# State-space heads: chunks along the free axis, two heads on the partition halves, two pairs multiplied in turn

## The reference

```python
proj = hidden @ W_in * mup_vector                  # 256 -> 1344
z, xBC, dt = split(proj, [512, 512 + 768])
xBC = silu(conv_b + causal 4-tap convolution of xBC along time)
x, Bm, Cm = xBC[:512] as 64 heads x 8, xBC[512:640], xBC[640:]
dt = softplus(dt + dt_bias)                        # one per head and step
dA = exp(dt * -exp(A_log))
state = state * dA_t + (dt_t * x_t) (outer) B_t    # per head: 8 x 128
y_t = state . C_t                                  # 512 steps, 64 heads
y = (y + D * x) * silu(z); y *= rsqrt(mean(y^2) + eps) * norm_w
out = y @ W_out
```

## Time and profile before

| | us |
|---|---|
| median of 3 runs | 1537.1 |
| the profiled execution, its own time | 1533.86 |
| its span, first to last instruction | 1532.1 |
| layer norm 2, 750 to 770 | 20 |
| projection stage, 770 to 884 | 114 |
| heads stage, 884 to 1229 | 345 |
| mean granted TensorE clock | 0.91 |

### The profile page before, as it was taken

How to read it: one execution, slowest core, us unless ns; L and a number is a source line. 1 busy time by engine, 2 the same in 40 slices (tenths; PEclk the granted TensorE clock), 3 DMA queues, 4 the chain that set the end, 5 groups by cost and what they waited for, 6 DMA issues and landing times. The chain is left out here.

```text
span 1532.1 us, 35054 instructions
## 1 busy us (share of the span) xinstructions
PE 1224.8 (80%) x13688; PEld 930.2 (61%) x13688; DVE 991.7 (65%) x2104; ACT 613.6 (40%) x1380; POOL 618.5 (40%) x540
## 2 busy tenths in 40 slices
PE   2789898988854999997168778989888846999992
PEld 1356665656542889886134336666666635989882
...
GB/s 149 148 133 155 186 163 168 169 181 151 122 67 139 420 341 235 248 220 43 154 1 3 12 15 2 2 3 2 2 2 2 2 84 324 415 233 251 234 123 175
DMA packets 93702, 209.91 MB, mean 137 GB/s; under 512 B 33057, under 2 KB 64546, under 8 KB 87394
## 3 DMA queue, kind: packets, MB, share of 16 engines
...
## 5 line engine op out<-in xcount | busy, mean ns | idle before, releaser
L1222 ACT ACTIVATE ffn_h<-ffn_bank,ffn_b 128x256 f32<-128x256 f32 (+1 forms) x384 | 144.2, 430 | 274.5 <-PE ffn_bank L118 267.5
L2208 POOL TENSOR_TENSOR ssm_GL<-ssm_L,ssml_G 128x512 f32<-128x512 f32 x128 | 164.7, 1295 | 109.7 <-DVE ssm_L L2117 109.7
L1399 DVE CAST ffn_hh<-ffn_h 128x512 f16<-128x512 f32 (+1 forms) x192 | 73.6, 383 | 179.0 <-ACT ffn_h L1222 169.8
L1034 POOL DMA_INDIRECT ffn_xs<-xn_rows,ffn_from_rows x78 | 78.2, 1003 | 266.3 <-PE ffn_bank L1117 180.8
L116 PE MATMUL ffn_bank<-ffn_hh,ffn_W 128*128 128x256 f16 (+1 forms) x768 | 180.2, 253 | 4.9 <-DVE ffn_hl L1401 4.9
L117 PE MATMUL ffn_bank<-ffn_hl,ffn_W 128*128 128x256 f16 (+1 forms) x768 | 180.0, 252 | 0.0
L118 PE MATMUL ffn_bank<-ffn_hh,ffn_W 128*128 128x256 f16 (+1 forms) x768 | 180.0, 252 | 0.0
L1973 PE MATMUL ssm_Y<-ssm_GL,ssmh_windows 64*32 64x64 f32 x4096 | 145.5, 223 | 9.4 <-POOL ssm_GL L2208 9.0
L2117 DVE TENSOR_TENSOR_SCAN ssm_L<-ssm_bank,ssmh_ident 128x512 f32<-128x512 f32 x128 | 151.1, 1210 | 0.8 <-PE ssm_bank L1956 0.8
L1973 PEld LDWEIGHTS ssm_Y<-ssm_GL,ssmh_windows 64*32 64x32 f32 x4096 | 124.6, 111 | 38.1 <-issue 24.7
L642 ACT ACTIVATE att_prob<-att_bank,att_nmax 128x512 f32<-128x512 f32 (+3 forms) x256 | 127.2, 525 | 29.4 <-DVE att_nmax L724 28.1
...
...
## 6 DMA issues: line engine op xcount, KB each, us to landing
...
att_piece<-in_ffn_w SPq DMA_DIRECT2D x32, 512.0 KB, 5.0
split_w<-att_halves SPq DMA_DIRECT2D x32, 512.0 KB, 4.3
...
ffn_back<-y_rows SPq DMA_DIRECT2D x16, 512.0 KB, 7.3
att_KB<-att_krl SPq DMA_DIRECT2D x8, 512.0 KB, 5.5
...
xn_rows<-ffn_XN SPq DMA_DIRECT2D x8, 512.0 KB, 2.6
```

What stands on the lines that cost most here:

```text
L1222: ins_ = act.activation(h[layer][:, m, 0:n], bank[1 + 2 * layer + u][:, (m % 2) * n:(m % 2 + 1) * n], ACT.Gelu, bias=bias[:, ds(e + m, 1)])
L2208: pool.tensor_tensor(GL[:, p % RING, :, :, :].rearrange("p x i n -> p x (i n)"), L[:, p % RING, :, :, :].rearrange("p x i n -> p x (i n)") ...
```

## The change

Heads stage. The eight chunks of time now lie along the free axis, and the two halves of the partitions hold the two heads of a pair. So a product in `multiply` runs over all 128 rows. `multiply` is called for every second p and takes two pairs at once, with products of 128 rows x 32 columns that alternate between two column groups. `scan` writes into one ring of 6 slots (4 new, 2 in the no longer needed `FT`), and `mult` works in place there. `windows` has 3 slots and is filled by two ACT instructions for each pair. `update` becomes two products of half the width on the two halves of the partitions, in two banks. The tables `finishes` and `outputs` have other numbers.

Projection stage. x, dt and the suffix decays now have to come out with head halves on the partitions. The transposes become ordinary float32 products with picked columns of the identity, 64 x 64 each, and `multiply_g` is cut into 64 x 64 pieces too. B is stored to DRAM by SP and loaded again in the heads stage, in the new layout. The weights are permuted on the host to match. The decays go to `piece` by 8 DMAs instead of 32.

Elsewhere. In `layer_norm_stage` DVE normalises group g + 1 before the low parts of group g - 1. In `ffn_stage` SP waits for the gathered rows of tile 0 before it loads the second part of the first expert, and for those of tile 1 before it goes on to the other experts.

```diff
             statistics(1)
+            normalise(0)
             for g in range(G):
-                normalise(g)
                 if g + 2 < G:
                     statistics(g + 2)
+                if g + 1 < G:
+                    normalise(g + 1)
...
                     sp.dma_start(to[:, :, 0:W2_AT], src[:, :, 0:W2_AT]).then_inc(first_in, 16)
+                    sp.wait_ge(xs_loaded[0], 32)
                     sp.dma_start(to[:, :, W2_AT:], src[:, :, W2_AT:]).then_inc(weights[0], 16)
+                    sp.wait_ge(xs_loaded[1], 32)
...
                 for i in range(TB):
-                    one = slice(i * P, (i + 1) * P)
-                    ins = pe.matmul(bank[7][:, one], bc[:, one], CT[:, b * TB + i, :], start=True, stop=True)
+                    for par in range(2):
+                        at = slice((2 * i + par) * CH, (2 * i + par + 1) * CH)
+                        for x in range(2):
+                            ins = pe.matmul(bank[7][half(x), at], bc[:, at], CT[:, b * TB + i, par * CH:(par + 1) * CH], start=True, stop=True)
                 ins.then_inc(s["g_psum"], 1)
...
-                    for c in range(XB):
-                        ins = pe.transpose(bank[5 + i % 2][:, c * P:(c + 1) * P], xc[:, c, i * P:(i + 1) * P], identf[:, :])
+                    for par in range(2):
+                        for c in range(XB):
+                            at = (par * XB + c) * CH
+                            for x in range(2):
+                                ins = pe.matmul(bank[5 + i % 2][half(x), at:at + CH], xc[:, c, i * P + par * CH:i * P + (par + 1) * CH],
+                                                channels[:, x, :, :], start=True, stop=True)
                     ins.then_inc(s["xt_psum"], 1)
...
+            def turn_by_heads(rows, before, chunks_read):
 
                 pe.wait_ge(s["xt_done"], 2 + chunks_read)
                 pe.wait_ge(s["turned"], before)
                 for r in range(PAIRS):
+                    for c in range(2 * TB):
+                        for x in range(2):
+                            ins = pe.matmul(bank[5 + r][half(x), c * CH:(c + 1) * CH], rows[:, r * S + c * CH:r * S + (c + 1) * CH],
+                                            heads[:, x, :, :], start=True, stop=True)
+                    ins.then_inc(s["turn_psum"], 1)
+
...
+            def store_b(b):
+                sp.wait_ge(s["b_done"], b + 1)
+                sp.dma_start(b_rows[b].rearrange("(i p) n -> p i n", p=P), Bt[:, :, :]).then_inc(s["b_stored"], 16)
+
+            def spread_halves(part, src):
+                for r in range(PAIRS):
+                    for bb in range(2):
+                        sp.dma_start(piece[part * SH:(part + 1) * SH, 2 * r + bb, :], src[bb * SH:(bb + 1) * SH, r, :]).then_inc(s["pieces"], 16)
+
+            for b in range(B - 1):
+                store_b(b)
+            sp.wait_ge(s["hi_done"], 1)
+            spread_halves(0, hi16)
+            sp.wait_ge(s["lo_done"], 1)
+            spread_halves(1, lo16)
+            store_b(B - 1)
+            sp.wait_ge(s["pieces"], 4 * PAIRS * 16)
+            sp.wait_ge(s["b_stored"], 16 * B)
+
...
-    RING, WINDOWS = 3, windows.shape[1]
+    RING, WINDOWS, YB = 6, windows.shape[1], 3
...
-        L, GL = sb("L", [P, RING, 2, TB, CH]), sb("GL", [P, RING, 2, TB, CH])
-        edtx, states = sb("edtx", [P, 2, SD]), sb("states", [P, NC - 1, SD])
+        L = sb("L", [P, RING - B // 2, S])
+        slots = [L[:, n, :] for n in range(RING - B // 2)] + [FT[:, r, :] for r in range(B // 2)]
+        Bt = sb("Bt", [P, 2, NC, P])
+        edtx, states = sb("edtx", [P, 2, 2, SD // 2]), sb("states", [P, NC - 1, SD])
         carried = sb("carried", [P, S - CH])
...
-        Y = ctx.enter_context(nc.psum_tensor("ssm_Y", [P, 4, 2, TB, CH], F32))
-        bank = t.banks(4)
+        Y = ctx.enter_context(nc.psum_tensor("ssm_Y", [P, YB, NC, CH], F32))
+        U = ctx.enter_context(nc.psum_tensor("ssm_U", [P, 2, S], F32))
+        bank = t.banks(3)
...
-        finishes = {PAIRS_B * b + at: (b, q) for b in range(B) for q, at in enumerate((19, 23, 40, 44) if b + 1 < B else (19, 23, 33, 34))}
-        outputs = {PAIRS_B * b + (49 if b + 1 < B else 39): b for b in range(B)}
+        finishes = {PAIRS_B * b + at: (b, q) for b in range(B) for q, at in enumerate((11, 19, 27, 35) if b + 1 < B else (11, 19, 27, 34))}
+        outputs = {PAIRS_B * b + (41 if b + 1 < B else 39): b for b in range(B)}
...
+            def load_b(b):
+                if b >= 2:
+                    sp.wait_ge(upd_psum, (b - 1) * (NC - 1))
+                for x in range(2):
+                    sp.dma_start(Bt[half(x), b % 2, :, :], b_rows[b].rearrange("(c t) n -> t c n", t=CH)).then_inc(bt_loaded[b % 2], 16)
...
-                for x in range(2):
-                    group, h = divmod(2 * m + x, SH // 2)
-                    ins = pe.matmul(bank[p % 2][:, x * TB * CH:(x + 1) * TB * CH], picks[:, h, :], piece[:, b, group, :], start=True, stop=True)
-                ins.then_inc(bc_ready, 1)
+                q, group, h = place(m)
+                pe.matmul(bank[p % 2][:, :], picks[:, q * PAIRS_Q + group * 2 + h, :], piece[:, b, :], start=True, stop=True).then_inc(bc_ready, 1)
...
-                if jj == 0 and q % 2 == 0 and b:
-
-                    pe.wait_ge(y_read, (b - 1) * XB + q + 2)
-                pe.wait_ge(window_done, p + 1)
-                pe.wait_ge(mult_done, p + 1)
-                for x in range(2):
-                    j = 2 * jj + x
-                    at, out_rows = AT - j % 4 * SP_, slice(j // 4 * GROUP, (j // 4 + 1) * GROUP)
-                    for i in range(TB):
-                        for par in range(2):
-                            rows = rows_of(par)
-                            ins = pe.matmul(Y[out_rows, q // 2 * 2 + par, q % 2, i, :], windows[rows, p % WINDOWS, x, i, at:at + GROUP],
-                                            GL[rows, p % RING, x, i, :], start=j % 4 == 0 and i == 0, stop=j % 4 == 3 and i == TB - 1)
+                q, _, h = place(m)
+                at = b * XB + q
+                if m % PAIRS_Q == 0 and at >= YB:
+
+                    pe.wait_ge(y_read, at - YB + 1)
+                pe.wait_ge(window_done, p + 2)
+                pe.wait_ge(mult_done, p + 2)
+                for c in range(NC):
+                    for n in range(2):
+                        group = place(m + n)[1]
+                        ins = pe.matmul(Y[group * GROUP:(group + 1) * GROUP, at % YB, c, :],
+                                        windows[:, (p + n) % WINDOWS, c, (1 - h) * SP_:(1 - h) * SP_ + GROUP],
+                                        slots[(p + n) % RING][:, c * CH:(c + 1) * CH], start=h == 0 and c == 0, stop=h == 1 and c == NC - 1)
                 ins.then_inc(y_done, 1)
 
             def update(b, c):
                 i, par = divmod(c, 2)
+                if c == 0:
+                    pe.wait_ge(bt_loaded[b % 2], (b // 2 + 1) * 32)
                 pe.wait_ge(edtx_done, b * TB + i + 1)
                 fourth_free()
-                pe.matmul(bank[3][:, :], Bt[rows_of(par), b * TB + i, :], edtx[rows_of(par), (b * TB + i) % 2, :], start=True,
-                          stop=True).then_inc(upd_psum, 1)
+                for x in range(2):
+                    ins = pe.matmul(U[:, x, 0:SD // 2], Bt[half(x), b % 2, c, :], edtx[half(x), (b * TB + i) % 2, par, :], start=True, stop=True)
+                ins.then_inc(upd_psum, 1)
                 used["update"] += 1
...
-                if 1 <= p <= NP:
-                    multiply(p - 1)
+                if 2 <= p <= NP and p % 2 == 0:
+                    multiply(p - 2)
...
-                    act.wait_ge(y_done, p - WINDOWS + 1)
-                act.activation(windows[:, p % WINDOWS, :, :, AT:AT + SP_].rearrange("p x i d -> p i x d"),
-                               dtx[:, b * TB:(b + 1) * TB, m * 2 * SP_:(m + 1) * 2 * SP_].rearrange("p i (x d) -> p i x d", x=2),
-                               ACT.Copy).then_inc(window_done, 1)
+                    act.wait_ge(y_done, (p - WINDOWS) // 2 + 1)
+                q, group, h = place(m)
+                at = (q * PAIRS_Q + group * 2 + h) * SP_
+                chunks = dtx[:, b * TB:(b + 1) * TB, :].rearrange("p i (a d) -> p (i a) d", a=2)
+                for x in range(2):
+                    ins = act.activation(windows[half(x), p % WINDOWS, :, (2 * x + 1) * SP_:(2 * x + 2) * SP_],
+                                         chunks[half(x), :, at:at + SP_], ACT.Copy)
+                ins.then_inc(window_done, 1)
...
-                    dve.wait_ge(mult_done, p - RING + 1)
-                dve.tensor_tensor_scan(flat(L[:, p % RING, :, :, :]), bank[p % 2][:, :], ident8[:, :], 0.0, ALU.mult,
+                    dve.wait_ge(y_done, (p - RING) // 2 + 1)
+                dve.tensor_tensor_scan(slots[p % RING], bank[p % 2][:, :], ident8[:, :], 0.0, ALU.mult,
```

(13 more changed lines are left out.)

171 lines of the change are left out of this document (92 added, 79 removed).

## The result

The changed kernel is slower: 1618.5 us (median of 4 runs, 1615.81 to 1620.21) against 1536.3, a ratio of 1.053 with a 95% interval of 1.050 to 1.056. The forecast was 1498. The profiled execution of the changed kernel has a span of 1616.0 us, 83.9 more than before.

What follows compares the result with a forecast made beforehand. In the heads, the loop through PE, DVE and POOL was taken to set the pace, not PE alone. Heads -41, projection +16, layer norms -6, FFN -6 gave -37 from the profiled 1533.9; forecast 1498 us, range 1462 to 1532.

Steps and rivals of the forecast that it cites:

- Layer norm: Layer norms 0 and 2: ACT's waits for DVE's shift go with DVE's order turned, -4.5 and -1.5, together -6 us.
- Mixtures of experts: FFN: weight loads put behind the gathers shorten PE's waits for gathered rows, -2.5 and -3.5, together -6 us.
- Projection: Projection stage: 33 us more PE work at 55 to 66 ns a turn_x record, partly covered, +16 us.
- Heads: Heads stage: two full batches -18, start -10, rest of batch 0 -5, last batch -8, together -41 us.
- the carry: Heads, carry period of two pairs: one round takes 5.5 us instead of 5.3; four in a full batch are 22.
- the update: Heads, update period of two pairs: falls from 4.37 to 3.5 us, what DVE needs; seven are 24.5, with squares 25.
- rival D: Heads: PE's clock stays at 0.50 through the stage, as PE is busy less; 1575 us, 6% chance.
- B: Heads: column groups do not run side by side, multiply takes 1.7 to 2.05 for two pairs; 1525 us, 15% chance.
- C: turn_x and multiply: load and product of a full-row record come one after the other; 1577 us, 6% chance.
- Rival E: Heads: deeper ring removes handovers, DVE and POOL set the pace, 60 us a batch; 1461 us, 15% chance.
- the eight pairs behind them: Heads, full batch: eight pairs after the four carry periods, with both halves of project, take 17.5 us.
- the rest: Heads, end of a full batch after the updates: 6.5 us, 6.1 before, by the later window.

Runs made afterwards that it cites:

- e_ln_ffn: Kernel before, with only DVE's new order in the layer norms and SP's two waits in the mixtures of experts: 1525.6 us against 1532.4.
- e_keep: Changed kernel with keep_decay ahead of window(p + 2) in ACT's order, nothing else changed: 1567.7 us.
- e_late_only: Changed kernel with spread(p + 2) behind multiply and update on PE in the even passes, nothing else changed: 1575.8 us.
- e_before_half: Kernel before with half of multiply's products left out, those of the second head of each pair: 1556.0 us against 1536.8.
- e_order: Changed kernel with keep_decay ahead of window and the even spread behind multiply and update, no idle products: 1519.4 us.
- e_same_group: Changed kernel with keep_decay ahead of window, three idle products a pass, and multiply doing one column group after the other: 1565.6 us in one run.
- The fastest version: Changed kernel with keep_decay ahead of window, even spread behind multiply and update, and two idle PE products a pass: 1511.5 and 1514.4 us.
- e_fill2_again: Repeat with more rounds: changed kernel, keep_decay ahead of window, even spread behind multiply and update, two idle PE products a pass: 1514.4 us.

## Why the prediction was wrong

**The sum by its terms.** Layer norm -6 forecast, -5.0 measured up to the end of attention, and in layer norm 2, where -1.5 was counted, nearly nothing (from the first gathered rows to the projection -0.5). Mixtures of experts -6 forecast; -1.2 and, with the wait 2.6 shorter, -2.3 measured. Projection +16 forecast, +4.6 measured: the 55 to 66 ns for a record were too high. The lower end of 32 ns, which stood in the range, is what records on alternating column halves cost (2.09 us for 64). `multiply` at 1.09 and `update` at 0.70 (0.64 in pitch) were right at the upper clock. Heads: -41 forecast, +88 measured. That is the miss; the other terms together came out 8 us better than forecast. The weights and the gathers are not on the same queue, as the prediction had it: SP starts the one (`ffn_W`, 46 loads of 2048 KB), POOL the other (`ffn_xs`, 78 gathers), and the 20.46 MB that q0 moved before are what the 156 gathers and scatters of POOL come to (an estimate, 128 rows of 1 KB each), beside 185.11 MB on q1. That the waits get shorter when the loads are held back is what the runs show (8.27 and 9.40 us before, 7.07 and 6.79 in the changed kernel, 7.63 and 7.14 in e_ln_ffn).

**The step that failed first** is the carry: "One round is scan 1.15, `mult` 1.24, `multiply` 1.06, two `window` ... 5.5 instead of 5.3". The prediction had seen that the `window` ahead of `keep_decay` waits for `multiply`. It had not asked what stands ahead of that `multiply` on PE: the carry itself and two spreads. With the rows of before, `carry` is 1.67 and its two products some 0.4, the spreads 0.33 each. The row then is spread 0.33, carry 1.9, spread 0.33, multiply 1.02, windows and `keep_decay` 1.1, `read_inter` 0.55, scan 1.15, which is 6.4 at the upper clock, an estimate, and 9.67 as measured at the lower one. `mult`, which the forecast's round had, is not in it. e_keep took the chain away, brought the period from 9.67 to 5.03, and gave 51 us.

**The second** is the update: "The period of two pairs falls ... to what DVE needs, ... 3.5, as PE's path from the end of a scan ... then fits". It does not fit, since PE runs spread(p + 2), which waits for the scan of this very pass, ahead of `multiply`. The listing of the order ahead of the prediction shows it: L2012 above L2027 in each pass. The period was 5.1 on average in the changed kernel (1165.82 to 1191.51), 4.36 with the clock up and the carries repaired, and 4.09 with the spread moved as well; e_late_only gave 43 us. So the step was mis-sized besides: DVE's block of output, which it did not count, and the sums of squares, for which it added 0.5 us to all seven, are part of what keeps it above 3.5.

**The third** is the clock. It was rival D, with 6%, and priced at 1575 by PE's work alone. Its sign was right and its weight too small, for two reasons. "Stayed up through carries in which PE waits" was taken from before, where PE was busy 17.5 of 20 us in the carries, at 1.00 (980 to 1000); after, it was 13.9, at 0.50 (1000 to 1020). And D was priced apart from the chains, while here they go together: with a chain in it the stage had a lower clock than without (0.66, 0.69 and 0.73 against 0.81, all without idle products), and at the lower level `multiply` is 1.8 times as long (1.92 us against 1.08), as is the row of `carry` (3.09 against 1.67). e_before_half shows the clock with no chain added (+19 us), e_order shows the chains without help for the clock (0.66 to 0.81 by itself). What in PE's work brings the level down is not shown: PE was busy 26.0 of 26 us at 0.50 at the start of the stage before, and 18.4 of 24 us at 1.00 in e_order (1140 to 1164).

**Rivals B and C** fall. Alternating column groups did run side by side: a record costs 32 ns in turn and 53 ns one after the other (e_same_group). The forecast had taken this as its author's estimate, since no row of before shows two column groups at once. e_same_group shows what B would have cost too, 1.71 for two pairs, as B had it. C would also have cost more than its 1577: at its own 3.5 us for two pairs PE has some 92 us of work in a full batch of 80 (an estimate: B's 53, with 16 calls at 3.5 instead of 1.06), where the sum counted 5 us for the whole stage. C had load and product of a record one after the other when both have all rows. That does not hold here: all 128 rows are used by each of these records, and they cost 32 ns on alternating column groups, with the loads busy for 0.93 us of a row of 1.09 us:

```profile
1191.51 0.93 PEld L2027 LDWEIGHTS ssm_Y<-ssml_FT,ssmh_windows 128*32 128x32 f32 x32 [0.23 <-issue]
```

Rival E counted 60 us for a full batch; the changed kernel had 105 and more, and with both chains repaired it was never below 75. (Its sum is off by 2 besides: 16 but for 5 is 11, and 9 were taken off.)

**What the forecast had too small even without the chains.** The fastest version took 1511 to 1514 us. The forecast, with what was measured for projection, layer norms and mixtures in place of its own terms, would be 1490. The missing part is in the heads: -14 in e_fill2_again where -41 was forecast. By part of the stage, cut at the first `read_inter` of each batch:

| us | before | forecast | changed | e_order | e_fill2_again |
|---|---|---|---|---|---|
| start of the stage to batch 1 | 97.1 | 82.1 | 112.4 | 94.8 | 90.7 |
| batch 1 | 80.2 | 71.0 | 112.4 | 79.8 | 77.2 |
| batch 2 | 80.2 | 71.0 | 105.1 | 77.0 | 75.3 |
| batch 3 and the tail | 94.6 | 86.6 | 110.3 | 95.2 | 94.8 |

And by the terms of the prediction for a full batch, cut at `multiply` (batch 1 and 2):

| us | forecast | changed | e_order | e_fill2_again |
|---|---|---|---|---|
| four carry periods | 22 | 36.6, 35.6 | 18.5, 19.4 | 19.8, 18.7 |
| the eight pairs behind them | 17.5 | 26.1, 26.4 | 20.9, 20.4 | 20.5, 20.0 |
| seven updates | 25 | 40.1, 35.7 | 31.2, 31.4 | 28.5, 28.5 |
| the rest | 6.5 | 9.6, 7.4 | 9.2, 5.8 | 8.0, 8.0 |

In e_fill2_again the granted clock of these two batches is 0.96 and 0.98, so these are hardly the clock. They hold its two idle products a pass, some 0.9 us of PE's work in each period (an estimate, four of 0.22); e_order has none, but a lower clock, and is no shorter in these two terms. The carries came out better than forecast, and the updates and the pairs with `project` worse by some 3 us each.

**What is left open.** Why the last batch gave nothing, where -8 was forecast, no run took apart. At the start of batch 0 DVE is busy 9.93 of 10 us (894 to 904, e_order and e_fill2_again alike), so that stretch gives nothing either.
